# Third edge stage of a four-layer graph kernel: three engine programs as loops over the row buffers

## The chip, the cores and the metric

The kernel runs on one core of a Trainium2 chip. The time is that of one execution on the device, in microseconds (us), as the median of several runs. Five engines work side by side, each through its own list of instructions: TensorE (PE, matrix products), VectorE (DVE), ScalarE (ACT), GpSimd (POOL, which issues the gathers here) and SyncE (SP, which issues plain transfers). They meet only at semaphores: one adds to a counter, another waits until the counter has a value. An engine has a sequencer, which reads instructions and handles register arithmetic, branches and some waits itself, and a datapath behind it.

## The reference, cut to what matters

A graph has 6,250 nodes of 128 channels and 206,250 edges, sorted by target node. Four layers follow one another. The change touches the edge part of the third one:

```
h = relu(layernorm(x))                                  # 6250 x 128
xs, xv = h[:, :32] @ W_up0, (h[:, 32:] as 32x3) @ W_up1 # node tables
emb = radial basis of edge_weight                       # 8 numbers an edge
w = silu(silu(emb @ w0 + b0) @ w1 + b1) @ w2 + b2       # 4 x 32 weights an edge
Y = sqrt(3) * edge_vec / |edge_vec|
m0 = w0 * xs[src];  m1 = w1 * xs[src] * Y
m2 = w2 * xv[src];  m3 = w3 * <xv[src], Y> / sqrt(3)
sums over the edges of each dst of (m0, m3) and of (m1, m2)   # 256 numbers a node
```

## The kernel before, in words

The kernel is written engine by engine, with the semaphores set by hand; nothing reorders it. Edges are taken in tiles of 128 and groups of U = 4 tiles. There are EDGE_GROUPS = 403 groups. `table2` in device memory has a row of 128 numbers for each node. R = 4 row buffers hold the gathered rows of a group each, so that group n uses buffer r = n mod 4 and turn g = n div 4 of the buffers.

For every group n of the third edge stage:

- SP (L1607) waits until the messages of group n-4 are done (`s_mid`, which starts at 4) and loads the radial basis of the group into `base`. Its program is already a loop over the turns (`ring`, L90).
- POOL (L1618) waits for the same count and issues four indirect gathers, one for each tile, into `rows` (L1623).
- TensorE, `radial` (L1695): `w0` times `base` (L1699), the bias product (L1700), `w1` times `h1` (L1703), then four products with `w2` that give the edge weights in `psW` (L1707). It does so for group n+2 while it sums group n: `sums` (L1710) multiplies `mid` with the one-hot matrix `hot`, two products for each of the four tiles (L1714), into `psS`. Products in f32 stand as several instructions, each with a load of weights ahead of it.
- ScalarE (L1631): two Silu operations, `h1` (L1633) and `h2` (L1635), each between two products of TensorE.
- VectorE, `messages` (L1652), for group n+1: the one-hot matrix `hot` (L193), the products and sums that give `mid` (L1664 to L1680), and between them the four `add`s of group n (L1650): each reads the sums of a tile from `psS` and adds them to `ACC` at the window of 128 nodes that begins with the tile's first dst. These four node numbers are loaded into registers (L200), and the place in `ACC` is worked out in registers.

So the sums of group n on TensorE need `mid` of group n and `hot` of group n from VectorE, and the adds of group n on VectorE need these sums. The program of TensorE runs `step` (L1717) for n = 0 to 402, after `radial` for groups 0 and 1; that of VectorE runs `messages(0)` and then its `step` (L1682).

The words `ring` and `straight` are two helpers. Both call `step(n, g, r)` for every n. In `straight` (L110) n is a Python number, so that the program has 403 copies of the step, one behind the other, with constants as the values to wait for and as the addresses. In `ring` (L90) there is one loop over g on the engine, whose body has 4 copies of the step, for r = 0 to 3. There n and g come from a register. As 403 is 4 x 100 + 3, the loop makes 100 turns and three steps stand behind it.

Of the kernel before, what the change touches and what calls it, by code (L numbers as in the profile page):

```python
# [26 lines left out]
EDGE_GROUPS = -(-E // (P * U))  # L27
# [62 lines left out]
def ring(eng, total, slots, step):  # L90

    with eng.Fori(0, total // slots) as g:
        for r in range(slots):
            step(slots * g + r, g, r)
    for n in range(total - total % slots, total):
        step(n, n // slots, n % slots)
# [13 lines left out]
def straight(total, slots, step):  # L110

    for n in range(total):
        step(n, n // slots, n % slots)
# [7 lines left out]
def build(nc, a, out):  # L121
# [19 lines left out]
    with ctx:  # L141
# [9 lines left out]
        def alloc(stack):  # L151
# [12 lines left out]
            return sb, ps, sem  # L164

        sb, _, _ = alloc(ctx)

        def pool_sems(name, n):
# [29 lines left out]
        def windows(eng, tile):  # L198

            _, firsts = nc.values_load_multi_w_load_instructions(  # L200
                D0[0:1, bass.ds(tile, U)], engines=(eng.engine,), min_val=0, max_val=N,
                skip_runtime_bounds_check_because="a dst is a node number, and padding edges end at N")
            return firsts
# [368 lines left out]
        with ExitStack() as st:  # L572
            sb, ps, sem = alloc(st)
            R0 = H * B0
            R = 3
# [330 lines left out]
        with spanning:  # L906
# [4 lines left out]
            with second:  # L911
# [131 lines left out]
                with ExitStack() as st:  # L1043
                    sb, ps, sem = alloc(st)
                    R = 3
# [436 lines left out]
            with third:  # L1482
# [99 lines left out]
                with ExitStack() as st:  # L1582
                    sb, ps, sem = alloc(st)
                    R = 4
# [17 lines left out]
                    with nc.Block() as block:  # L1602
# [26 lines left out]
                        @block.scalar  # L1629
                        def _(act):  # L1630
                            def silus(n, g, r):  # L1631
                                act.wait_ge(s_h0, n + 1)
                                nc.scalar.activation(h1[:, :], psA[:, 0, :], ACT.Silu, bias=b01[:, 0:1]).then_inc(s_h1, 1)  # L1633
                                act.wait_ge(s_h1p, n + 1)
                                nc.scalar.activation(h2[:, r % 2, :], psA[:, 1, :], ACT.Silu, bias=b01[:, 1:2]).then_inc(s_h2, 1)  # L1635

                            straight(EDGE_GROUPS, R, silus)

                        @block.vector
                        def _(dve):  # L1640
# [48 lines left out]
                                    messages(n + 1, g if r < R - 1 else g + 1, (r + 1) % R, n)  # L1689

                            messages(0, 0, 0)
                            straight(EDGE_GROUPS, R, step)

                        @block.tensor
                        def _(pe):  # L1695
                            def radial(n, g, r, between=(lambda: None, lambda: None)):

                                pe.wait_ge(s_base[r], 16 * g + 16)
                                nc.tensor.matmul(psA[:, 0, :], w0[:, :], base[:, r, :], start=True, stop=True).then_inc(s_h0, 1)  # L1699
                                nc.tensor.matmul(psW[:, r % 2, :, :], three[:, :], b2row[:, :].unsqueeze(1).to_broadcast([P, U, P]), start=True, stop=False)  # L1700
                                between[0]()
                                pe.wait_ge(s_h1, n + 1)
                                nc.tensor.matmul(psA[:, 1, :], w1[:, :], h1[:, :], start=True, stop=True).then_inc(s_h1p, 1)  # L1703
                                between[1]()
                                pe.wait_ge(s_h2, n + 1)
                                for u in range(U):
                                    done = nc.tensor.matmul(psW[:, r % 2, u, :], h2[:, r % 2, (u % 2) * P:(u % 2 + 1) * P], w2[:, u // 2, :], start=False, stop=u == U - 1)  # L1707
                                done.then_inc(s_w, 1)

                            def sums(n, r, tiles):  # L1710
                                for u in tiles:
                                    pe.wait_ge(s_free, n * U + (u + 1))
                                    for b in range(2):
                                        done = nc.tensor.matmul(psS[:, u, b, 0:P], mid[:, r % 2, u, b * C:(b + 1) * C], hot[:, r % 2, u, :], start=True, stop=True)  # L1714
                                    done.then_inc(s_sum, 1)

                            def step(n, g, r):  # L1717
                                pe.wait_ge(s_hot, n + 1)
                                pe.wait_ge(s_mid, n + (R + 1))
                                if isinstance(n, int) and n + 2 > last:  # L1720
                                    sums(n, r, range(U))
                                else:
                                    radial(n + 2, g if r < R - 2 else g + 1, (r + 2) % R,
                                           (lambda: sums(n, r, range(0, U // 2)), lambda: sums(n, r, range(U // 2, U))))

                            radial(0, 0, 0)
                            radial(1, 0, 1)
                            straight(EDGE_GROUPS, R, step)


        closing = ExitStack()
        with closing:
# [56 lines left out]
            with ExitStack() as st:  # L1789
                sb, ps, sem = alloc(st)  # L1790
                R = 4
# [393 lines left out]
```

## Time and profile before

| | us |
|---|---|
| median of 3 runs | 11154.02 (11152.67 to 11200.2) |
| the profiled execution, its own time | 11197.17 |
| its span, first to last instruction | 11195.4 |
| from 5898 to 8614 us: the third edge stage | 2716 |
| TensorE busy in that stretch | 2069.93 |
| VectorE busy in that stretch | 1827.50 |
| GpSimd busy in that stretch | 1583.76 |
| ScalarE busy in that stretch | 382.88 |

The times are in microseconds from the start of the span. Register, branch and semaphore instructions, and the issue of a transfer, are not counted as busy. "PE" is a matrix product and "PEld" a load of weights; the start of a product is recorded and its end is modelled. A clock (PEclk) of 1.00 is the higher of TensorE's two levels, 2.4 GHz, and 0.50 the lower one, 1.2 GHz. A row of waits names who was idle, on which tile and line, and what seems to have ended the idle time. Where that is "DMA HN" or "DMA relB" within this stage, the name comes from another stage that used the same semaphore, and "remote" and "issue" name nobody. A number of packets in a queue called "instruction" is that of the blocks of code which engines read from device memory.

### The profile page before, as it was taken

The numbers are of one execution on the slowest core, as the hardware profiler recorded it, in microseconds if no ns is written. First come the engines' busy times: TensorE is split into PE (matmuls) and PEld (weight loads), VectorE is DVE, ScalarE is ACT, GpSimd is POOL, SyncE is SP. The second block draws the span as 40 slices with busy tenths as digits, with TensorE's granted clock in tenths as the row PEclk, the third lists the DMA queues.
The fourth block names the chain that finished last, engine by engine and source line by source line (L and its number), as shares of the span: only waits on it lengthen the run. The fifth ranks groups of instructions, "written<-read, shape, count | busy, mean of one in ns | idle before, by whom it ended". The sixth has DMA issues, their size and how long they took to land. (4 is left out here: it accounts for less than half of the span.)

```text
span 11195.4 us, 158258 instructions
## 1 busy us (share of the span) xinstructions
PE 7512.2 (67%) x45679; PEld 5676.2 (51%) x45679; DVE 6853.5 (61%) x18737; ACT 4365.1 (39%) x7367; POOL 7061.2 (63%) x6167
## 2 busy tenths in 40 slices
PE   1333333335899998998956777777777677777775
PEld 1322322333666666666645666666666344444443
DVE  3555555566677777666655666666666444444445
ACT  1111121121667776666621111111111566666664
POOL 3666666662688888888855555556554655555554
PEclk5555555556889999999977888888888788888887
DMA  4434434442666666777761111111111111111111
GB/s 118 110 96 105 111 98 104 101 97 65 103 106 106 107 106 109 109 109 109 110 117 46 43 43 43 43 42 43 42 42 46 45 43 44 44 44 45 44 44 43
DMA packets 1068830, 846.48 MB, mean 76 GB/s; under 512 B 404136, under 2 KB 907183, under 8 KB 1067542
## 3 DMA queue, kind: packets, MB, share of 16 engines
q0 software_dynamic: 360512, 407.88, 20.9%
q1 hardware_dynamic: 676812, 313.54, 12.7%
q10 hardware_dynamic: 30652, 115.04, 3.1%
q8 instruction: 368, 6.03, 0.2%
q14 instruction: 486, 3.98, 0.1%
HBM read 696.14 MB, written 139.60 MB: 75 GB/s over the span
## 5 line engine op out<-in xcount | busy, mean ns | idle before, releaser
L1474 POOL DMA_INDIRECT sums<-sumrows,index x1460 | 2458.1, 1684 | 694.3 <-issue 348.9
L1623 POOL DMA_INDIRECT rows<-table,index x1612 | 1583.8, 982 | 1128.8 <-DVE mid L1680 582.1
L679 POOL DMA_INDIRECT rows<-table,index x1612 | 1609.3, 998 | 1015.9 <-issue 692.0
L1873 POOL DMA_INDIRECT ACC<-table,index x1472 | 1398.4, 950 | 1129.2 <-DVEq L1998 615.1
L1650 DVE TENSOR_TENSOR ACC<-ACC,psS 128x256 f32 x1612 | 674.6, 418 | 792.1 <-PE psS L1714 471.2
L1714 PEld LDWEIGHTS psS<-hot,mid 128*128 128x128 f32 x6448 | 1042.9, 230 | 57.7 <-issue 3.0
L1714 PE MATMUL psS<-hot,mid 128*128 128x128 f32 x6448 | 1032.2, 313 | 2.7 <-DVE mid L1680 2.3
L2045 PE MATMUL psG<-limbs,pickA 128*128 128x384 bf16 x4060 | 902.1, 355 | 159.4 <-issue 102.7
L1910 ACT ACTIVATE pickA<-apart,K 128x512 bf16<-128x512 bf16 x1015 | 721.2, 711 | 717.2 <-remote 475.0
L1966 DVE TENSOR_TENSOR pickD<-ACC,psK 128x512 bf16<-128x512 f32 x700 | 459.9, 682 | 746.4 <-remote 545.4
L1421 PE MATMUL psB<-pickD,limbs 128*128 128x512 bf16 (+1 forms) x2964 | 824.5, 391 | 81.5 <-DVE pickD L1288 77.0
L1421 PE MATMUL psB<-pickA,limbs 128*128 128x512 bf16 (+1 forms) x2964 | 820.9, 389 | 28.1 <-ACT pickA L1355 24.1
L1954 DVE TENSOR_TENSOR ACC<-ACC,psS 128x128 f32 x1612 | 464.1, 288 | 470.7 <-remote 188.9
L1903 ACT ACTIVATE apart<-ACC,lows 128x512 bf16<-128x512 f32 x1015 | 732.4, 722 | 33.5
L1707 PE MATMUL psW<-w,h 128*128 128x128 f32 x3224 | 503.0, 305 | 351.4 <-ACT h L1635 205.1
L2045 PE MATMUL psG<-limbs,pickD 128*128 128x384 bf16 x2800 | 651.2, 350 | 119.3 <-issue 116.1
L1633 ACT ACTIVATE h<-psA,b 128x256 f32<-128x256 f32 x403 | 190.7, 473 | 1319.8 <-PE psA L1699 775.0
L2045 PEld LDWEIGHTS psG<-limbs,pickA 128*128 128x128 bf16 x4060 | 415.2, 105 | 484.8 <-issue 210.1
L1347 ACT ACTIVATE apart<-steps,away 128x512 bf16<-128x512 int16 (+1 forms) x988 | 646.5, 694 | 7.0
L1707 PEld LDWEIGHTS psW<-w,h 128*128 128x128 f32 x3224 | 454.1, 217 | 379.5 <-ACT h L1635 220.3
L829 DVE TENSOR_TENSOR ACC<-ACC,psA 128x128 f32 x1612 | 465.7, 289 | 286.5 <-issue 101.2
L1355 ACT ACTIVATE pickA<-apart,K 128x512 bf16<-128x512 bf16 (+1 forms) x988 | 638.5, 684 | 0.1
(349 smaller groups left out, 15303.0 us busy)
## 6 DMA issues: line engine op xcount, KB each, us to landing
win<-table SPq DMA_DIRECT2D x1612, 64.5 KB
srow<-src_f SPq DMA_DIRECT2D x365, 256.0 KB
HN<-rel_f ACTq DMA_DIRECT2D x102, 512.0 KB
relB<-rel_f ACTq DMA_DIRECT2D x102, 512.0 KB
rows<-table,index POOLq DMA_INDIRECT x3224
er<-limbs SPq DMA_DIRECT2D x1632, 3.0 KB
ACC<-table,index POOLq DMA_INDIRECT x1472
sums<-sumrows,index POOLq DMA_INDIRECT x1460
```

Of the source, the lines that this page charges most:

```text
L679: nc.gpsimd.indirect_dma_start(out=rows[:, r, k, :], out_offset=None, in_=table0[:, :], in_offset=bass.IndirectOffsetOnAxis(ap=index[:, n ...
L1347: nc.scalar.activation(apart[:, at % 2, 0:size], steps16[:, 0:size], ACT.Abs, bias=away[:, m % 2, u, j:j + 1], scale=-1.0).then_inc(s_apar ...
L1421: last = nc.tensor.matmul(psB[:, c % 2, 0:size], limbs[:, m % 2, k, u, :], chosen, start=u == 0 and k == 0, stop=u == U - 1 and k == 2)
L1474: nc.gpsimd.indirect_dma_start(out=sums1[u][:, :], in_=sums[:, n % 2, u, :], in_offset=None, compute_op=ALU.add, out_offset=bass.IndirectO ...
L1623: nc.gpsimd.indirect_dma_start(out=rows[:, n % R, u, :], out_offset=None, in_=table2[:, :], in_offset=bass.IndirectOffsetOnAxis(ap=index[: ...
L1650: nc.vector.tensor_tensor(own, own, psS[:, u, :, 0:P], ALU.add).then_inc(s_free, 1)
L1707: done = nc.tensor.matmul(psW[:, r % 2, u, :], h2[:, r % 2, (u % 2) * P:(u % 2 + 1) * P], w2[:, u // 2, :], start=False, stop=u == U - 1)
L1714: done = nc.tensor.matmul(psS[:, u, b, 0:P], mid[:, r % 2, u, b * C:(b + 1) * C], hot[:, r % 2, u, :], start=True, stop=True)
L1873: nc.gpsimd.indirect_dma_start(out=rows[:, n % R, u, :], out_offset=None, in_=table3[:, :], in_offset=bass.IndirectOffsetOnAxis(ap=index[: ...
L1903: nc.scalar.activation(apart[:, at % 2, :], names[:, m % 2, :], ACT.Abs, bias=lows[:, onA[k]:onA[k] + 1]).then_inc(s_apart, 1)
L1910: nc.scalar.activation(pickA[:, at % RING, :], apart[:, at % 2, :], ACT.Relu, bias=K[:, C1:C1 + 1], scale=-1.0).then_inc(s_pickA, 1)
L2045: done = nc.tensor.matmul(psG[:, u, 0:3 * C], chosen[:, u * P:(u + 1) * P], limbs[:, b, :], start=b == 0, stop=b == TN - 1)
```

## The change

In the third edge stage, and only there, the programs of TensorE, VectorE and ScalarE call `ring` in place of `straight`. SP's was a loop before. POOL's stays written out. The arithmetic, the tiles and the order of the products are the same.

```diff
@@ ScalarE
-                            straight(EDGE_GROUPS, R, silus)
+                            ring(act, EDGE_GROUPS, R, silus)
@@ VectorE
                             messages(0, 0, 0)
-                            straight(EDGE_GROUPS, R, step)
+                            ring(dve, EDGE_GROUPS, R, step)
@@ TensorE
                             radial(0, 0, 0)
                             radial(1, 0, 1)
-                            straight(EDGE_GROUPS, R, step)
+                            ring(pe, EDGE_GROUPS, R, step)
```

The rows below are instructions in the order of the program, with the line, the operation and the tiles. An ISA row is several register operations in one instruction, a REGISTER_ALU row is one of them; plain waits for semaphores have no row of their own. On VectorE, the start of a group before:

```order
L193 TENSOR_TENSOR hot<-K,REL 128x512
L1664 TENSOR_TENSOR dot<-rows,unit 128x384
L200 TENSOR_LOAD D
L1667 TENSOR_TENSOR q_2<-psW,rows 128x128
L1650 ISA
L1650 TENSOR_TENSOR ACC<-ACC,psS 128x2x128
L1670 TENSOR_TENSOR dot<-dot 128x4x32
```

and in the changed program, from the top of the loop to just ahead of the same first add:

```order
L92 ISA
L193 TENSOR_TENSOR hot<-K,REL 128x512
L1656 ISA
L1663 REGISTER_ALU
L1664 ISA
L1664 TENSOR_TENSOR dot<-rows,unit 128x384
L200 ISA
L200 TENSOR_LOAD D
L1666 REGISTER_ALU
L1667 TENSOR_TENSOR q_2<-psW,rows 128x128
L1647 REGISTER_ALU
L1648 REGISTER_ALU
```

Behind these come the same ISA row and add of L1650. Values to wait for (L1663, L1666, L1647, L1648) and addresses (L193, L1664, L200) are now worked out on the way. From the `L92 ISA` row to the branch at the end the body has 131 rows. Its end, with the first row behind it:

```order
L1678 TENSOR_TENSOR mid<-psW,rows 128x4x32
L1680 TENSOR_TENSOR mid<-psW,dot 128x4x32
L1648 REGISTER_ALU
L1650 ISA
L1650 TENSOR_TENSOR ACC<-ACC,psS 128x2x128
L92 REGISTER_ALU
L92 COMPARE_AND_BRANCH
```

On TensorE, a group before and the end of the body now; "x4" and "x2" are products with nothing between them:

```order
L1699 MATMUL psA<-base,w_2 128x256
L1700 MATMUL psW<-b2row,three 128x512
L1714 MATMUL psS<-hot,mid 128x128 x4
L1703 MATMUL psA<-h_2,w_2 128x256
L1714 MATMUL psS<-hot,mid 128x128 x4
L1707 MATMUL psW<-w_2,h_2 128x128 x4
```

```order
L1712 REGISTER_ALU
L1714 MATMUL psS<-hot,mid 128x128 x2
L1707 MATMUL psW<-w_2,h_2 128x128 x4
L92 REGISTER_ALU
L92 COMPARE_AND_BRANCH
```

The products keep their order; register rows stand between them (28 rows of registers and branch in the body), and a branch behind the fourth group. On ScalarE the body has 15 rows; its top is

```order
L92 ISA
L1633 ACT_TABLE_LOAD
L1633 ACTIVATE h_2<-psA,b_2 128x256
L1635 ACTIVATE h_2<-psA,b_2 128x256
L1632 REGISTER_ALU
```

Before, the load of the activation table stood once, ahead of the first Silu. Now it stands at the top of the body, and so is issued in each of the 100 turns.

## Rows read from the trace of the kernel before

**Rows 1.** Busy time by windows, third edge stage: PE, PEld, DVE, ACT, POOL, PEclk, DMA
```profile
5898.00:8614.00 2716.00, 2069.93 (x11687) 1737.54 (x11687) 1827.50 (x5241) 382.88 (x807) 1583.76 (x1612) 0.83 0.16 43
```
**Rows 2.** Groups of instructions there: count, busy us, mean ns, idle before and releaser
```profile
L1623 POOL DMA_INDIRECT rows<-table,index x1612 | 1583.8, 982 | 1128.8 <-DVE mid L1680 582.1 <-issue 524.0 <-DMA index<-in_src_cols 22.7
...
L1714 PE MATMUL psS<-hot,mid 128*128 128x128 f32 x6448 | 1032.2, 313 | 2.7 <-DVE mid L1680 2.3 <-issue 0.4
L1650 DVE TENSOR_TENSOR ACC<-ACC,psS 128x256 f32 x1612 | 674.6, 418 | 792.1 <-PE psS L1714 471.2 <-DMA HN<-rel_f 260.4 <-issue 54.2
...
L1633 ACT ACTIVATE h<-psA,b 128x256 f32<-128x256 f32 x403 | 190.7, 473 | 1319.8 <-PE psA L1699 775.0 <-remote 308.9 <-issue 236.0
```
**Rows 3.** Waits in that stretch: total us, times, longest us
```profile
POOL rows L1623 <- DVE mid L1680: 582.1, 188, 7.8
...
DVE ACC L1650 <- PE psS L1714: 471.2, 393, 4.8
...
DVE ACC L1650 <- DMA HN<-rel_f: 260.4, 204, 6.2
...
DVE ACC L1650 <- issue: 54.2, 88, 3.4
```
**Rows 4.** Timeline, three groups: start, us, what, idle before
```profile
7003.96 0.69 DVE L193 TENSOR_TENSOR hot<-K,REL 128x512 f32<-128x512 f32 x1
...
7004.64 1.05 PE L1714 MATMUL psS<-hot,mid 128*128 128x128 f32 x8
...
7007.65 0.42 DVE L1650 TENSOR_TENSOR ACC<-ACC,psS 128x256 f32 x1 [2.33 <-PE psS L1714]
...
7012.32 0.69 DVE L193 TENSOR_TENSOR hot<-K,REL 128x512 f32<-128x512 f32 x1
...
7013.70 1.92 PE L1714 MATMUL psS<-hot,mid 128*128 128x128 f32 x8
...
7018.64 0.68 DVE L193 TENSOR_TENSOR hot<-K,REL 128x512 f32<-128x512 f32 x1
...
7023.65 0.69 DVE L193 TENSOR_TENSOR hot<-K,REL 128x512 f32<-128x512 f32 x1
```
**Rows 5.** Windows in and between these groups, columns as in rows 1
```profile
7000.00:7004.00 4.00, 3.61 (x28) 3.37 (x29) 3.69 (x13) 0.95 (x2) 3.08 (x4) 1.00 0.16 41
...
7012.00:7018.00 6.00, 5.82 (x22) 4.93 (x23) 4.32 (x13) 0.95 (x2) 3.84 (x4) 0.50 0.13 36
```
**Rows 6.** SP's loop, line L92: instructions in the queue, ns min/median/max
```profile
L92 SPq FUSED_REGOPS  x100: 2/50/716, 5899.2 to 8543.3; - x100
L92 SPq ALU_OP  x100: 8/33/712, 5901.6 to 8569.6; - x100
L92 SPq COMPARE_BRANCH  x100: 3/45/698, 5901.7 to 8569.7; - x100
```
**Rows 7.** The page: its head, and the queues of code (packets, MB, share)
```profile
span 11195.4 us, 158258 instructions
...
q8 instruction: 368, 6.03, 0.2%
q14 instruction: 486, 3.98, 0.1%
```
**Rows 8.** The same two queues in the stage, 5898 to 8614 us
```profile
q8 instruction: 93, 1.52, 0.2%
q14 instruction: 94, 0.77, 0.1%
```
**Rows 9.** Issues of the whole program: KB each, median us from issue to landing
```profile
WX<-in_L_gnn_lin_w SPq DMA_DIRECT2D x2, 64.0 KB, 1.9
...
WT<-in_L_gnn_W ACTq DMA_DIRECT2D x1, 64.0 KB, 3.2
```
**Rows 10.** TensorE's own wait at a group's start, line L1698, ns min/median/max
```profile
L1698 PEldq EVENT_SEMAPHORE  x401: 406/1535/4653, 5912.7 to 8596.7; - x134
```
**Rows 11.** Groups of instructions of line L1633: the table load
```profile
L1633 ACT ACT_TABLE_LOAD x1 | 1.3, 1283 | 12.9 <-PEq L144 12.9
```

## The prediction

> **What bounds the kernel now.** I read the busy time by windows first, for the stage that the change touches. It lasts 2716 us for 403 groups, 6.74 us a group, and no engine fills it: TensorE 2070 us (76%), VectorE 1828 (67%), GpSimd 1584 (58%), ScalarE 383 (14%). TensorE's granted clock is 0.83 there, so it has the lower level, 1.2 GHz, for about a third of the time [rows 1].
>
> The groups of instructions and the waits tell what the idle time is. GpSimd needs 982 ns for a gather and 524.0/1612 = 0.33 us between two, so 4 x 1.31 = 5.23 us a group, and it waits for VectorE's `mid` 188 times, 582 us in all [rows 2, 3]. It is a floor of 403 x 5.23 = 2110 us, but not the bound. VectorE idles almost only ahead of its adds: 471 + 260 + 54 = 786 us, in 393 + 204 + 88 = 685 waits [rows 3]. In program order only the sums of L1714 can hold an add, so all three names stand for them. TensorE idles for `mid` and for ScalarE. So the bound is a circle: `mid` of VectorE, sums of TensorE, adds of VectorE, `mid` of the next group. Whatever delays either engine at a group's start delays all of it.
>
> The timeline shows that the groups differ. From 7018.64 to 7023.65 one takes 5.0 us. The one from 7003.96 takes 8.4: TensorE's sums are recorded from 7004.64, as fast as ever, but VectorE's add gets its first result so late that it starts at 7007.65, after 2.33 us. I can't say from this why. The next one, from 7012.32, takes 6.3 us with the sums at 1.92 us in place of 1.05 [rows 4]. Its window has a clock of 0.50, where 7000 to 7004 has 1.00 [rows 5]. So a late circle leaves TensorE idle, the clock falls, and the next group is slow as well.
>
> **The change part by part.** Values and arithmetic stay. Four things change.
>
> *Register instructions.* In the body VectorE has 131 instructions for four groups. Before, it had 18 rows a group in the order, and five plain waits which that list leaves out. Nearly all of the new ones come ahead of waits, while VectorE's datapath still works on what it has: between an add and the next add there are 0.6 to 1.6 us of queued operations. What can't hide is the register work of L1648 and L1650 behind a late result. SP's loop shows a register operation at 33 ns and a fused one at 50 [rows 6]. I take 0.05 us for each of the 685 waits that something ended late: 34 us. It is 0 if GpSimd's floor takes it, and 685 x 0.1 = 69 us at most. TensorE's register rows stand between products whose waits sit in the queue, and it is ahead: it waits a median of 1535 ns for `mid` at a group's start, and 406 at the least [rows 10]. Seven or so of 33 to 50 ns are 0.3 us and hide there: nothing, or 403 x 0.1 = 40 us without that cover.
>
> *The branch back.* SP's costs 45 + 33 + 50 ns, 0.13 us a turn [rows 6], but its body is short, four loads with their registers. The question is whether the top of the body is still in the engine when the branch goes there. The code comes from device memory in blocks: 6.03 MB in 368 packets is 16.4 KB each (q8), 3.98 MB in 486 is 8.2 KB (q14), and together 10.0 MB over 158,258 instructions is 63 bytes each [rows 7]. TensorE alone can need the large ones: 2 x 11,687 products and loads of weights in the stage are 58 a group [rows 1], 23,374 in all, and 93 packets of q8 at 16.4 KB and 63 bytes hold 24,200 [rows 8]. So VectorE's body of 131 instructions is 8.3 KB, a little more than its block, and TensorE's, 4 x 58 and 28 more, is 260 instructions and 16.4 KB, a block again. Both cross from one block into another in each turn, wherever they start. The code comes in order now, and no trace here shows an engine going back over a block's edge. If the next block takes the place of the one that the branch goes back to, it must be read again while the engine stands still. The price is then that of a small transfer: 1.9 us is the shortest of the 64 KB ones, 3.2 another [rows 9].
>
> The Trainium skill has both halves of this ("Runtime: NRT & Kernel Launch", on instruction fetch mechanics). A taken branch whose target is outside the two pages that the engine holds must wait for a DMA fetch. But it gives TensorE 128 KB and the others 32 KB, and by these sizes both bodies would fit. The packets of 8.2 KB in this trace are half of its 16 KB page. By its sizes the result would be my first rival, by its window of two pages it depends on where the prefetch stands.
>
> For VectorE I take 1.9 + 0.13 and subtract the add that still runs when the branch is read, 0.42 us [rows 2]: 1.6 us a turn. For TensorE it is 1.9 to 3.2 less its lead of 1.5 [rows 10], so 0.5 to 1.8, and at the same moment, since its next step needs the `mid` that VectorE has just finished. Side by side they cost 1.6 a turn, 160 us in 100 turns. The ends are 100 x 0.13 = 13 us (nothing is read again) and 100 x (3.2 + 0.13) = 333 us with no cover at all.
>
> *The clock.* An idle TensorE at each turn's end meets the lower level more often. Such a group takes 6.3 us against 5.0 [rows 4]. If the fall comes in addition in 60 of 100 turns, as many already fall without it, that is 60 x 1.3 = 78 us. The ends are 0 and 100 x (8.4 - 5.0) less the 1.6 of stall, 180 us.
>
> *ScalarE's table load*, 1283 ns [rows 11], now in every turn. ScalarE is idle 1319.8/403 = 3.3 us ahead of each first Silu [rows 2], and the load doesn't wait for TensorE. The idle time hides it: nothing. Without the cover it would be 128 us.
>
> *What goes.* 187 blocks of straight code [rows 8]. No wait names them, VectorE has no idle time elsewhere than at its adds, and if code is read again there are more packets, not fewer. Nothing; at best a tenth of a microsecond each, -19 us.
>
> Sum: 34 + 160 + 78 = 272 us. The profiled execution took 11197.17 us, 1.8 more than its span, and would take 11469. It stands 43 us above the median of 11154, near the slowest of the three; I add to the median: 11426, so 11430 us (+2.5%).
>
> **The rivals.** *Both bodies stay in the engine.* For it: SP's loop has no long branch at the median, a body is only just over a block, and two blocks may well be held. Against it: nothing in this trace. The registers and 0.13 us a turn remain, 34 + 13 = 47 us: 11200. This is the case to which the Trainium skill's memory sizes lead.
>
> *Two stalls in a row.* If TensorE's reload doesn't lie beside VectorE's, because one waits for the other's first result, a turn costs 1.6 + 1.8 = 3.4 us, and with the upper ends of the clock (180) and registers (69): 340 + 249 = 590 us, 11740. For it: the circle. Against it: TensorE comes to its branch 1.5 us early.
>
> *Faster, through the late sums.* The group of 8.4 us waits for results that TensorE seems to have made. If that hangs on the pattern of waits in TensorE's queue, which register instructions now break up, or on the reading of code, fewer groups would be late. GpSimd's floor allows 2716 - 2110 = 606 us at most. A fifth of it, 120 us, less 47: 11080. It decides from 47 us saved, which is 14 late groups of 3.4 us. For it: the cause is open. Against it: late groups come every three to four groups, code blocks of TensorE every 2716/93 = 29 us [rows 8], which is 4.3 groups.
>
> **How the numbers follow.** Reload with overlap 0.50, resident bodies 0.27, stalls in a row 0.13, faster 0.10. A measurement of this kernel tells 0.5%, 56 us, from no change. Resident bodies at +47 with 0 to 120 us fall on both sides: 0.17 within, 0.10 above. So faster 0.10, the same 0.17, slower 0.73. The forecast's own range is 11290 (13 + 34 + the clock, with a reload mostly covered) to 11620. The range for all reaches down to the resident case and up towards the second rival: 11180 to 11700.
>
> **What would show it.** Reload: q8 in the stage at 200 packets or more and q14 at 200 or more, in place of 93 and 94; on VectorE an idle time of 1 to 2 us ahead of L193 in every fourth group, where the idle time now is nearly all ahead of L1650; PEclk in the stage below 0.83. Resident: fewer than 20 packets in both together, and idle time only ahead of L1650. Stalls in a row: TensorE idle ahead of L1699 for over 3 us in every fourth group. The registers: more idle time ahead of L1650, in shares of 0.05 us. The table load: 101 of them at 1.28 us, with ScalarE's L1633 never late by it. I would be wrong if the stage got shorter than 2716 us, or if the idle time sat at every group and not at every fourth.

## The result, and the profile after

The changed kernel took 11286.2 us (median of 4 runs, 11265.24 to 11305.74). The kernel before, run beside it, took 11165.69 us (4 runs, 11152.67 to 11200.2). The ratio is 1.0100, with a 95% interval of 1.0082 to 1.0118: 120 us slower by the medians, 92 to 132 by that interval. The forecast was slower by 272 us. The sign was right, the size was more than twice too large, and the step that made it large, the reading of code at each branch back, did not take place. The time lies inside the forecast range (11180 to 11700).

The page's head and its two queues of code answer to [rows 7]:

```profile
span 11268.0 us, 165461 instructions
...
q8 instruction: 277, 4.54, 0.2%
q14 instruction: 409, 3.35, 0.1%
```

There are 7203 instructions more in the trace, and 168 packets of code fewer. The same two queues within the stage, 5898 to 8687 us, answer to [rows 8]:

```profile
q14 instruction: 17, 0.14, 0.0%
q8 instruction: 2, 0.03, 0.0%
```

93 and 94 packets have become 2 and 17. The prediction asked for fewer than 20 in both together if the bodies stay in the engines, and for 200 in each queue if they are read again. It is the first: 19.

Busy time by windows (PE, PEld, DVE, ACT, POOL, PEclk, DMA share, GB/s) for the part ahead of the stage, the stage, and the part behind it; the second row answers to [rows 1]:

```profile
0.00:5898.00 5898.00, 3575.01 (x23425) 2727.30 (x23426) 3754.34 (x10613) 2454.91 (x4116) 4087.22 (x3103) 0.75 0.56 105
5898.00:8687.00 2789.00, 2124.21 (x11640) 1776.12 (x11638) 1818.83 (x5222) 505.93 (x899) 1561.31 (x1593) 0.82 0.15 40
8687.00:11268.00 2581.00, 1856.82 (x10616) 1210.03 (x10616) 1277.91 (x2904) 1531.89 (x2451) 1397.39 (x1472) 0.83 0.17 45
```

The part behind the stage is as long as it was (11195.4 - 8614 = 2581 us). The stage takes more. Its window holds 401 of the 403 groups (VectorE's `hot` is counted below), so a group takes 2789/401 = 6.96 us, against 6.74: 0.22 us by 403 groups is 89 us. Measured between the starts of L1664, from the first group to the last, it is 6.965 against 6.698 us, 107 us. The spans differ by only 73 us, because in this profiled execution the stage begins 30 us earlier (5868 in place of 5898), in work that the change doesn't touch. The profiled execution also had the highest mean granted clock of the four (0.782, the others 0.774 to 0.777).

Groups of instructions in the stage (count, busy us, mean ns, idle before and what ended it) answer to [rows 2] and [rows 11]:

```profile
L1623 POOL DMA_INDIRECT rows<-table,index x1593 | 1561.3, 980 | 1211.4 <-DVE mid L1680 699.4 <-issue 512.0
...
L1714 PE MATMUL psS<-hot,mid 128*128 128x128 f32 x6432 | 1051.8, 318 | 2.7 <-DVE mid L1680 2.3 <-issue 0.4
L1650 DVE TENSOR_TENSOR ACC<-ACC,psS 128x256 f32 x1610 | 667.9, 415 | 744.0 <-PE psS L1714 407.0 <-DMA HN<-rel_f 236.4 <-issue 95.1
...
L193 DVE TENSOR_TENSOR hot<-K,REL 128x512 f32<-128x512 f32 x401 | 274.3, 684 | 1.6
...
L1633 ACT ACTIVATE h<-psA,b 128x256 f32<-128x256 f32 x400 | 189.4, 474 | 1382.5 <-PE psA L1699 654.2 <-remote 592.5 <-issue 135.8
...
L1633 ACT ACT_TABLE_LOAD x99 | 127.0, 1283 | 1.8
L1667 DVE TENSOR_TENSOR q<-psW,rows 128x128 f32<-128x128 f32 x401 | 114.0, 284 | 227.5 <-DMA relB<-rel_f 223.2 <-PE psW L1707 2.8 <-issue 1.4
```

Of the kernel before, the row of L1667 in its stage and its wait:

```profile
L1667 DVE TENSOR_TENSOR q<-psW,rows 128x128 f32<-128x128 f32 x403 | 116.1, 288 | 77.7 <-DMA relB<-rel_f 70.9 <-PE psW L1707 4.6 <-issue 1.2
```
```profile
DVE q L1667 <- DMA relB<-rel_f: 70.9, 31, 5.5
```

Read these rows on VectorE, which holds the circle. Ahead of `hot` (L193), the first operation behind a branch back, it idles for 1.6 us in this window: there is no stall there. Ahead of the adds (L1650) it idles less than before, 744 us against 792. What is new stands ahead of L1667, the first product that needs TensorE's `psW`: 227.5 us, where before it was 77.7. The name of a DMA there is the profile's guess; by the program that wait is for TensorE's L1707. VectorE's idle time in the stage was about 893 us (792.1 + 77.7 + 14.2 + 8.7). Over the whole stage of the changed kernel, from 5868 us on, it is 1001 (749.9 + 227.5 + 13.5 + 10.3). The difference, 108 us, is the 107 us by which the stage is longer. So the loss is waiting for TensorE's results, and it stands in the groups of all four positions in a turn: between starts of L1664 they took 6.66, 6.85, 6.55 and 6.73 us before and take 6.81, 7.07, 7.01 and 6.98. A cost of the branch would stand in one of the four.

The load of ScalarE's table takes 1283 ns in each turn, and costs nothing that this row shows.

The waits of the stage answer to [rows 3]:

```profile
POOL rows L1623 <- DVE mid L1680: 699.4, 201, 6.3
...
DVE ACC L1650 <- PE psS L1714: 407.0, 319, 4.2
...
DVE ACC L1650 <- DMA HN<-rel_f: 236.4, 149, 7.3
DVE q L1667 <- DMA relB<-rel_f: 223.2, 120, 4.7
...
DVE ACC L1650 <- issue: 95.1, 139, 2.8
```

Late adds number 319 + 149 + 139 = 607 in place of 685, late L1667s 120 (31 before, 70.9 us). The timeline (start, us, what, idle before) shows one such group, to be read beside [rows 4]:

```profile
7022.99 0.69 DVE L193 TENSOR_TENSOR hot<-K,REL 128x512 f32<-128x512 f32 x1
7023.60 0.55 DVE L1664 TENSOR_TENSOR dot<-rows,unit 128x384 f32<-128x384 f32 x1
7023.71 1.05 PE L1714 MATMUL psS<-hot,mid 128*128 128x128 f32 x8
7027.31 0.29 DVE L1667 TENSOR_TENSOR q<-psW,rows 128x128 f32<-128x128 f32 x1 [3.15 <-DMA relB<-rel_f]
7027.35 0.47 ACT L1633 ACTIVATE h<-psA,b 128x256 f32<-128x256 f32 x1 [6.27 <-remote]
...
7027.88 1.22 PE L1703 MATMUL psA<-h,w 128*128 128x256 f32 x2 [3.11 <-issue]
7028.90 1.91 PE L1714 MATMUL psS<-hot,mid 128*128 128x128 f32 x8
```

TensorE's sums are recorded from 7023.71 at full pace. Yet VectorE and ScalarE both go on with results that they need from it only at 7027.3, within 0.04 us of each other. Then the granted clock is at its lower level (0.50 between 7028 and 7032), and eight products take 1.91 us. It is like the late group of the kernel before, but the results for L1667 and the first Silu, which were on time there, are late here as well.

The register work is now seen directly. Instructions of the queue (ns: min/median/max) at L92 answer to [rows 6], and the two lines of an add stand with them:

```profile
L92 PEldq COMPARE_BRANCH  x100: 76/208/233, 5920.4 to 8673.1; - x100
L92 DVEq ALU_OP  x100: 40/40/40, 5921.4 to 8674.4; - x100
L92 DVEq COMPARE_BRANCH  x100: 50/56/73, 5921.5 to 8674.5; - x100
...
L92 DVEq FUSED_REGOPS  x99: 98/98/98, 5921.8 to 8649.7; - x99
...
L1648 DVEq ALU_OP  x1598: 40/40/40, 5901.9 to 8673.5; - x200
...
L1650 DVEq FUSED_REGOPS  x1610: 46/46/53, 5901.9 to 8686.1; - x179
```

VectorE's branch costs 56 + 98 + 40 = 0.19 us a turn, and each add has one register operation more, the 40 ns of L1648; the 46 ns of L1650 were there before. TensorE's wait at a group's start [rows 10] now stands in several instructions of its queue, so its lead can't be read in the same way.

### The profile page after: what moved, and what is told of

Its sections match the earlier page's. It is cut to its first block and busy times, and to the rows that moved or that the text cites. A ratio compares the mean times of both kernels' runs of the same rounds, so it can differ in the third digit from the quotient of the medians.

```text
span 11268.0 us, 165461 instructions
## 1 busy us (share of the span) xinstructions
PE 7556.0 (67%) x45679; PEld 5713.4 (51%) x45679; DVE 6851.1 (61%) x18738; ACT 4492.7 (40%) x7466; POOL 7045.9 (63%) x6167
## 5 line engine op out<-in xcount | busy, mean ns | idle before, releaser
L1650 DVE TENSOR_TENSOR ACC<-ACC,psS 128x256 f32 x1612 | 668.8, 415 | 749.9 <-PE psS L1714 407.0
L1714 PEld LDWEIGHTS psS<-hot,mid 128*128 128x128 f32 x6448 | 1068.1, 235 | 62.1 <-issue 3.0
L1714 PE MATMUL psS<-hot,mid 128*128 128x128 f32 x6448 | 1055.6, 318 | 2.7 <-DVE mid L1680 2.3
L1633 ACT ACTIVATE h<-psA,b 128x256 f32<-128x256 f32 x403 | 190.8, 474 | 1393.8 <-PE psA L1699 658.8
L1707 PE MATMUL psW<-w,h 128*128 128x128 f32 x3224 | 517.9, 312 | 216.0 <-ACT h L1635 172.5
L2018 PE MATMUL psS<-ACC 128*128 128x128 f32 x2944 | 480.5, 306 | 181.8 <-issue 114.1
```

What stands on the lines that cost most here:

```text
L1650: nc.vector.tensor_tensor(own, own, psS[:, u, :, 0:P], ALU.add).then_inc(s_free, 1)
```

## The experiments

e1 to e8 ran on chips on which the kernel before takes about 9460 us; the first measurement and e9 to e18 on chips where it takes 11154 to 11306. Each ratio is to the kernel before on the same chip, beside the run. The record gives one chip number to e9 to e15, yet the kernel before took 11306 us beside e9 to e12 and 11167 beside e13 to e15; so ratios are compared, and times only within a group of runs.

**e1 to e5: which program, and does it cost everywhere?** Each line of the change alone, then the whole:

```
e1, e4:  -  straight(EDGE_GROUPS, R, step)      +  ring(pe, EDGE_GROUPS, R, step)
e2, e4:  -  straight(EDGE_GROUPS, R, step)      +  ring(dve, EDGE_GROUPS, R, step)
e3:      -  straight(EDGE_GROUPS, R, silus)     +  ring(act, EDGE_GROUPS, R, silus)
e5:      all three, the changed kernel
```

> Only TensorE's program is a loop; VectorE's and ScalarE's stay written out. All three loops together cost 120 us. Theory T (what TensorE's sequencer now does between products, and a wait that moved from the sequencer into the queue, shift its late results so that the clock falls more often): +70 to +110 us, with more time at the lower clock in the stage. Rival V (register work of VectorE behind late sums): 0 to +20. Rival A (the table load in each turn of ScalarE): 0. On record: register rows of TensorE hide, so 0 to +40.

> Only VectorE's program is a loop. Theory V: 34 to 69 us for the register operations behind late sums, as on record, up to +110 if they are all there is. Theory T: 0 to +20. Theory A: 0. If VectorE reads its code again at each branch: over 190 packets of q14 in the stage; the changed kernel had 17, so I expect under 20.

> Only ScalarE's program is a loop, with the activation table's load in each turn (1283 ns). Theory A: the load makes the first Silu of a turn late, +60 to +120 us. Theories T and V, and what is on record (3.3 us of idle time cover it): within 10 us of before.

> TensorE's and VectorE's programs are loops, ScalarE's stays written out: the changed kernel without the table loads. Theories T and V: +100 to +120 us, as much as the changed kernel. Theory A: 0 to +40. If the three costs only arise together, this tells whether ScalarE's has a part.

> The changed kernel once more, beside a kernel before on the same chip. In the runs of e1 to e4 the kernel before took 9459 us and its third edge stage went at GpSimd's pace, 5.04 us a group. Theory G (the cost of the loops only shows where VectorE and TensorE are the bound, through results of TensorE that come late; where the gathers are, they cover it): if the kernel before takes about 9460 here, the ratio is 0.999 to 1.002; if it takes about 11160, the ratio is about 1.01 and the groups with late results are there. Rival S (the +120 us are the sum of three programs' costs wherever it runs): +100 us at either level.

Measured: 1.0006 (0.9996 to 1.0015), 1.0009 (1.0000 to 1.0019), 1.0004 (0.9995 to 1.0014), 1.0006 (0.9996 to 1.0015), and 0.9991 (0.9980 to 1.0003) for the whole change. None costs a clearly measurable amount here. The stage of e1 and a part of e5's (windows, columns as above) and e5's waits of GpSimd say why:

```profile
5430.00:7480.00 2050.00, 1688.22 (x11687) 1443.06 (x11687) 1799.39 (x5240) 381.95 (x807) 1542.46 (x1612) 0.99 0.21 56
```
```profile
5480.00:7400.00 1920.00, 1568.77 (x11035) 1341.38 (x11034) 1747.17 (x4947) 482.97 (x856) 1455.94 (x1523) 1.00 0.21 55
```
```profile
POOL rows L1623 <- issue: 464.4, 1523, 0.3
```

The same stage takes 2050 us in place of 2716. The clock stays up, no result is late, and in e5 GpSimd's only idle time is its 0.3 us between two gathers (1523 times, never longer, never for `mid`). In e1 `mid` is named 326 times, never for more than 0.3 us. A group takes 5.05 us, and GpSimd's own work is 4 x (956 + 305) ns, 5.04 us. That is the floor that the prediction named (at 5.23 us, by gathers of 982 ns), here reached, and it hides the loops.

**e6 and e7: the bare toll.** The gathers of the stage are left out from group 4 on, so the sums read old rows and GpSimd sets no pace. e6 does it to the kernel before, e7 to the changed one.

```
-  for n in range(EDGE_GROUPS):                  +  for n in range(R):
-  dve.wait_ge(s_rows[r], 16 * U * g + 16 * U)   +  dve.wait_ge(s_rows[r], 16 * U)
```

> The kernel before with the gathers of the third edge stage left out from group 4 on (the four row buffers keep the rows of groups 0 to 3; the output isn't the reference's). GpSimd's floor of 5.04 us a group is gone, so the stage goes at the pace of the circle of VectorE and TensorE. Where TensorE's results are on time: 4.4 to 4.7 us a group, about 0.4 us less, 9300 us in all. If late results come from the gathers' transfers, none are left here, even where the kernel before takes 11160 us.

> The same with all three loops. Without the gathers' floor the bare cost of the loops can be seen against e6: by what is on record for registers and branches 34 + 13 = 47 us (0.12 us a group); if the load of the activation table shows, more at one group in four. Rival: nothing, since register work hides in both engines' queues. With theory S it would be 100 us.

Measured: 9242.77 us (ratio 0.9757, 0.9738 to 0.9776) and 9282.72 (0.9800, 0.9782 to 0.9819). The medians differ by 40 us, the groups (between starts of L1664) by 4.607 - 4.495 = 0.112 us, 45 us in all, spread over the four positions (4.594, 4.617, 4.569, 4.647). The prediction had put 34 + 13 = 47 us on registers and the branch without a reload. The sum agrees by luck: it was 0.05 us for each of 685 late waits, and here no result is late.

**e8 and e12: when does a body no longer stay?** All gathers are present; the three loops run over 16 groups in a turn (e8, 25 turns) and over 8 (e12, 50 turns, `turns=2`).

```
+  def long_ring(eng, total, slots, step, turns=4):
+      whole = total // (slots * turns)
+      with eng.Fori(0, whole) as k:
+          for i in range(slots * turns):
+              step(slots * turns * k + i, turns * k + i // slots, i % slots)
```

> The three loops with 16 groups in a body and 25 turns: VectorE's body has 506 instructions, 32 KB, TensorE's over 1000. The changed kernel read 17 + 2 blocks of code in the stage, so bodies of 8.4 and 16.8 KB stay in the engines. If 32 KB don't stay, q14 has 25 x 4 = 100 packets or more in the stage, and each branch shows its price as idle time ahead of L193: 1.9 to 3.2 us by what is on record. If they stay, under 25. The time: within 0.3% of the kernel before either way where the gathers are the bound.

> All gathers present; the three loops run over eight groups in a turn (two rounds of the row buffers), 50 turns, so that VectorE's body is twice as long as in the changed kernel, about 16 KB, and half as long as in the kernel with sixteen groups in a turn, which showed 155 packets of code on VectorE's queue and 2.57 us a branch ahead of the hot sum. If 16 KB still stays in the engine: fewer than 20 packets on that queue within the stage, no idle ahead of the hot sum, and the time of the kernel before within 0.1%. If it doesn't: 100 or more packets, 50 branches by about 2.6 us or 130 us of idle, of which GpSimd's pace hides most as it did with 25 branches: plus 0.2 to 0.7%.

e8: 1.0024 (1.0015 to 1.0034). Code queues and the `hot` (L203 there), 5480 to 7400 us:

```profile
q14 instruction: 155, 1.27, 0.2%
q8 instruction: 3, 0.05, 0.0%
```
```profile
L203 DVE TENSOR_TENSOR hot<-K,REL 128x512 f32<-128x512 f32 x376 | 256.0, 681 | 59.3 <-issue 59.3
```

Here the reload exists: 155 packets of 8.2 KB in that stretch, and 59.3 us of idle time ahead of the first operation behind the branch, 2.6 us for each of 23 turns. VectorE's body is 506 instructions, 32 KB at the 63 bytes of the prediction's count; TensorE's, twice as long, is not read again (3 packets). The stalls also bring the clock down: PEclk is 0.96 in that window, where e5 has 1.00, and 22 stretches at the lower level begin in it, in e5 none.

```profile
5480.00:7400.00 1920.00, 1612.61 (x10904) 1379.21 (x10903) 1688.12 (x4888) 385.89 (x775) 1461.63 (x1505) 0.96 0.21 55
```

e12 ran where results come late: 1.0100 (1.0079 to 1.0121), where 0.1% had been expected of a body that stays. Its rows for 5898 to 8700 us:

```profile
q14 instruction: 18, 0.15, 0.0%
q8 instruction: 2, 0.03, 0.0%
```
```profile
L203 DVE TENSOR_TENSOR hot<-K,REL 128x512 f32<-128x512 f32 x388 | 267.1, 688 | 9.9 <-PEq L154 8.7
```

With 256 instructions, 16 KB, VectorE's body stays. So the size of the body decides, with the limit between 16 and 32 KB for VectorE. And with half as many branches the kernel is about as much slower as with all of them (113 us by its ratio, 89 to 137, against 112 in the first measurement and 138 in e17): most of what it pays doesn't count turns, as half of it would be 56 to 69 us. A share of 10 us, half of VectorE's 0.19 us a turn, is too small to be seen in it.

**e9 to e11: whose toll?** The edit of e6, and one of the three loops in each.

> Leaves out the gathers of the third row stage from group 4 on (the sums read old rows), so that GpSimd's gathers no longer set the pace; of the three programs only VectorE's is a loop. The straight form without those gathers took 9243 us and 4.495 us a group, the form with three loops 9283 us and 4.607 us. Theory one, the toll is VectorE's registers (eight of its waits a group now compare with a register, and an update of one costs 40 ns or more ahead of a sum that follows at once): 4.58 to 4.61 us a group and 9275 to 9285 us. Theory two, the toll is TensorE's (its records show the longer wait, 190 us ahead of L1699 in place of few): 4.49 to 4.52 us a group and 9240 to 9255 us. Shared evenly: 4.54 and 9260 us.

> Leaves out the same gathers; only TensorE's program is a loop. Theory one (VectorE's registers carry the toll): 4.49 to 4.52 us a group, 9240 to 9255 us. Theory two (TensorE's registers and its branch back of 208 ns carry it): 4.58 to 4.61 us a group, 9275 to 9285 us. If both are on the one chain through the recurrence of buffers, the two kernels add to the whole: about 4.55 each.

> Leaves out the same gathers; only ScalarE's program is a loop, with its table load of 1.283 us in every turn. If the load is hidden in ScalarE's idle time, as predicted: 4.49 to 4.51 us a group, 9240 to 9252 us. If it is on the path once a turn: 1.28 us by 100 turns, 128 us at most, 9370 us, with the longer period in one of every four groups.

Measured: 10391.64, 10362.8 and 10369.05 us, with 4.611, 4.540 and 4.516 us between starts of L1664. The absolute times can't be held against e6's, which came from another chip, and these means can't either: each holds one group of 11 to 13 us at the start of the stage, where gathers are still there, and e6 has none. Without the first ten groups they are 4.583, 4.514 and 4.492 us, against 4.489 in e6 and 4.601 in e7. The written-out form on a chip of this kind (e18, below, no late results either) has 4.492, so the comparison between the chips holds. VectorE's loop makes most of the difference of 0.112 us: 0.094, or 38 us in 403 groups. TensorE's makes 0.025 (10 us) and ScalarE's 0.003 (1 us), and the three add up to 0.122. The expectations of e13 and e14 still took 0.116 and 0.045 from the means. The window of e6 and VectorE's wait for sums in it (5460 to 7200 us), then the same of e9 (5930 to 7740):

```profile
5460.00:7200.00 1740.00, 1588.43 (x11244) 1367.53 (x11242) 1711.38 (x5039) 367.23 (x775) 5.32 (x6) 1.00 0.02 5
```
```profile
DVE ACC L1650 <- PE psS L1714: 2.3, 6, 0.4
```
```profile
5930.00:7740.00 1810.00, 1618.25 (x11449) 1392.95 (x11449) 1747.72 (x5132) 374.07 (x790) 0.00 (x0) 1.00 0.02 4
```
```profile
DVE ACC L1650 <- PE psS L1714: 48.8, 297, 0.5
```

VectorE was 98% busy in e6 (1711.38 of 1740 us), so its register operations ahead of the adds show as gaps: 48.8 us over 395 groups is 0.12 us a group, enough for the 0.094. Two more things stand in that window: without gathers nothing is late, on a chip of the kind where with them some 30% of the groups are (in the trace of the kernel before 119 of 397 groups have a wait of VectorE over 2 us), and the granted clock is 1.00.

**e13, e14 and e16: one loop each, all gathers, late results present.** The kernels of e2, e1 and e3 once more.

> Only VectorE's program is a loop, all gathers present: asked again because the earlier answer came from a chip where GpSimd's pace of 5.04 us a group hid everything; on the chips where TensorE's results come late (6.7 us a group) the changed kernel pays 120 us. Without the late results VectorE's loop alone carries the whole bare toll (4.611 us a group against 4.607 with three loops and 4.495 with none). Theory one, the toll of 0.11 us a group on VectorE is what is given back more than twice where results come late: plus 0.8 to 1.2% (90 to 135 us). Theory two, the toll is passed on as it is: plus 0.4% (45 us), and the other 70 us belong to TensorE's or ScalarE's loop. On a chip with no late results: within 0.1%.

> Only TensorE's program is a loop, all gathers present. Theory one: its bare toll is 0.045 us a group (4.540 against 4.495), so plus 0.15 to 0.4% (18 to 45 us). Theory two, the lateness itself depends on TensorE's program (its waits stand in the instruction stream as register work in place of constants): plus 0.6% or more (70 us). On a chip with no late results: within 0.1%.

> Only ScalarE's program is a loop, all gathers present. VectorE's loop alone measured plus 0.73% (0.46 to 1.00) and TensorE's plus 0.44% (0.27 to 0.61) on a chip where TensorE's results come late; together 130 us, against 120 us for all three. Theory one, the shares add up and nothing is left for ScalarE: within 0.2% (its table load of 1.283 us stays hidden). Theory two, its own register waits (two a group, each often the last to end) cost too: plus 0.2 to 0.5%. On a chip with no late results: within 0.1%.

| kernel | ratio (95%) | us | bare toll, us |
|---|---|---|---|
| VectorE's loop (e13) | 1.0073 (1.0046 to 1.0100) | 81 | 38 |
| TensorE's loop (e14) | 1.0044 (1.0027 to 1.0061) | 49 | 10 |
| ScalarE's loop (e16) | 1.0007 (0.9995 to 1.0020) | 8 | 1 |
| all three (first, e17) | 1.0100, 1.0122 | 112, 138 | 45 |

The us are the ratio by the kernel before on that chip, the bare toll is the difference of e9, e10, e11 and e7 to e6's 4.489 us a group, by 403. ScalarE's table load and its waits cost nothing that can be measured. VectorE and TensorE each pay some 40 us more than their bare toll, and these shares add: 0.73 + 0.44 + 0.07 = 1.24%.

**e15: a mere delay in VectorE's program.** No loops; two fills of a 128x1 tile more in each group.

```
+  nc.vector.memset(fill[:, 0:1], 0.0)     ahead of add(before, firsts, 0)
+  nc.vector.memset(fill[:, 1:2], 0.0)     ahead of add(before, firsts, 2)
```

> No loops; VectorE's program has two fills of 128x1 more in each group (a fill of 128x1 took 59 ns in the trace of before, so 0.118 us a group, the bare toll of VectorE's loop), one ahead of the first late sum and one ahead of the third. Theory one, it is the delay that counts, whatever makes it: the same as with VectorE's loop alone, plus 0.8 to 1.2% where results come late. Theory two, the delay is passed on as it is: 47 us, plus 0.4%. Theory three, only the loops' registers and branch do it: within 0.2%. On a chip with no late results: within 0.1%, hidden by GpSimd's pace.

Measured: 1.0038 (1.0024 to 1.0051), 42 us of the 47 put in. This delay is passed on as it is. It isn't multiplied, so theory one fell, and VectorE's loop seems to cost more (81 us) than a delay of some 40 us; the two intervals overlap a little (51 to 112 us, 27 to 57 us), so this alone doesn't prove it. Against their bare tolls, VectorE's loop (51 us or more, bare 38), TensorE's (30 to 68 us, bare 10) and all three (92 us or more, bare 45) do cost more. One rival is not tested: the fills stand at two places of VectorE's program, the register operations ahead of every wait of two engines, and the place of a delay may matter as much as its kind.

**e17: the changed kernel on e16's chip.**

> All three loops and all gathers, the changed kernel, on one chip with ScalarE's loop alone. If the shares add up (81 us VectorE, 49 us TensorE, about nothing ScalarE): plus 1.0 to 1.3% (115 to 145 us) where results come late. If the loops overlap in their cost: plus 0.7 to 0.9%. On a chip with no late results: within 0.1%.

Measured: 1.0122 (1.0103 to 1.0140), as the sum of the shares foretold. Its waits, 5880 to 8700 us, repeat the first result's, and behind them stand those of TensorE's loop alone (e14, same stretch):

```profile
POOL rows L1623 <- DVE mid L1680: 748.6, 186, 6.1
...
DVE q L1667 <- DMA relB<-rel_f: 328.8, 137, 4.8
```
```profile
DVE ACC L1650 <- PE psS L1714: 426.9, 262, 4.5
DVE ACC L1650 <- DMA HN<-rel_f: 267.5, 156, 6.9
DVE ACC L1650 <- issue: 169.1, 201, 4.0
DVE q L1667 <- DMA relB<-rel_f: 54.7, 27, 5.4
```

In the same stretch the wait of L1667 is 101.5 us (80 times) with VectorE's loop alone and 54.7 (27 times) with TensorE's alone, no more than before; only together do they make it large. What TensorE's loop costs alone stands ahead of the adds: 426.9 + 267.5 + 169.1 = 864 us, against 786 before.

**e18: half of the gathers.** From group 4 on two of each group's four are left out, in the kernel before (those tiles read old rows).

```
-  for u in range(U):      +  for u in range(U if n < R else U // 2):
```

> Leaves out two of the four gathers of each group from group 4 on (those tiles read old rows); no loops. Where TensorE's results come late with all gathers (6.70 us a group) and never with none (4.5 us): if each gather is what makes the results late, half of them leave about half of the lateness, 5.4 to 5.8 us a group, 10640 to 10800 us; if the lateness needs GpSimd to be busy nearly all the time, it goes: 4.5 to 4.7 us a group, about 10340 us, with the granted clock at 1.00 through the stage. On a chip with no late results: 4.50 us a group, as with none.

Measured: 10363.02 us, 0.9182 (0.9166 to 0.9198). The stage's window:

```profile
5930.00:7700.00 1770.00, 1614.14 (x11429) 1389.47 (x11428) 1741.71 (x5124) 374.00 (x789) 809.92 (x788) 1.00 0.13 34
```

The lateness goes altogether with half of the gathers, not by half: 4.49 us a group, the clock at 1.00, where all gathers make 6.7 in the trace of the kernel before (between starts of L1664). GpSimd is busy for 46% of that window. Leaving out 798 gathers saved 929 us.

## Why the prediction was wrong

**What bounds the kernel** was read rightly: the circle of `mid`, sums and adds, with late results in it. GpSimd's floor was right too, if a little high (5.23 us a group, 5.04 in e5), and e1 to e5 stand on it.

**The branch back** is the step that failed: 160 of the 272 us, "if the next block takes the place of the one that the branch goes back to". It doesn't: 19 packets of code in the stage, 1.6 us of idle time ahead of L193. The error was to take a body that crosses a block's edge for one that must be fetched; bodies of two blocks and more are held. The stall itself exists, and had the right order of size, 2.6 us a turn in e8 against 1.6 assumed. On VectorE a body of 16 KB doesn't bring it and one of 32 KB does. The Trainium skill ("Runtime: NRT & Kernel Launch", on instruction fetch mechanics) gives 32 KB to VectorE and 128 KB to TensorE, and a stall when the target lies outside what is held. In the runs 8 and 16 KB stayed, 32 KB on VectorE did not, and TensorE's 64 KB did. These runs agree with the sizes for TensorE and for the short bodies, and I should have given them more than 0.27. The body of 32 KB (506 instructions by 63 bytes, 31.9 KB) would just have fitted by the size alone and was read again all the same; a block read ahead may take part of the room, which is not shown. What remains of the branch, 0.19 us a turn on VectorE, is 19 us at most. TensorE's, 208 + 50 + 32 ns, is 0.29 us a turn, where I had taken SP's 0.13.

**The registers** were put at 34 us, or 47 with the branch. Their bare cost is 45 us (e7 against e6), and 38 of it VectorE's, as said; but that agreement is luck, since it comes from the gaps ahead of adds with VectorE otherwise full, and not from late waits. For TensorE I took nothing, because it waits 1.5 us for `mid`: bare it is 10 us, which the cover nearly explains, but where results come late it is 49, above the 40 that I gave it without any cover. Why is not shown.

**The clock** was put at 78 us for 60 more falls at the branches. In the traces, between the first start of L1664 and the last, the lower level was granted for 889 us in 127 stretches before, and for 1020 us in 152 after. Work of TensorE at that level takes up to twice as long (eight products of L1714 took 1.05 us at the one and 1.91 at the other), so 131 us of it give back up to 65 us. That is the size of what is missing between 45 and 120 us, so this term was nearly right in size. Where a branch does stall, as in e8, the clock falls with it; here nothing stalls at the branch, so the mechanism of the term failed with the reload.

Nor does the clock tell the loops from a mere delay. The record has the mean granted clock of every run, and twice its distance from 1, by the span, is the time at the lower level in the whole program. It is longer than in the kernel before, run beside, by 78 us with e15's fills, 69 with TensorE's loop, 128 with VectorE's, 15 with ScalarE's and 219 with all three (e17). These are 1.4 to 1.9 times the losses of 42, 49, 81, 8 and 138 us. More time at the lower level goes with every loss, and these runs can't say which of the two makes the other. So the part above the bare toll, some 65 to 95 us of all three loops' cost, stays without a shown cause. Where it sits is known: in waits for TensorE's results, ahead of L1667 and the first Silu with all three loops, ahead of the adds with TensorE's alone.

**The table load** at nothing: right, within what e11 and e16 can tell. **The blocks of code gone** at nothing: e1 to e5 agree.

**The rivals.** "Both bodies stay in the engine" was the right mechanism, at 47 us, and is what a chip without late results would show if GpSimd didn't hide it. "Two stalls in a row" fell with the reload. "Faster, through the late sums" was wrong in sign: of 397 groups, 119 had a wait of VectorE over 2 us before and 125 have one now, and those with one over 3 us went from 28 to 54. About as many groups are late, and some are later. The last sentence of the prediction named what would refute it, idle time at every group, and that is what came.

## What to carry to other kernels

A loop on an engine costs code fetches only when its body is larger than the engine holds: count the body's instructions by 63 bytes, and look at the packets of the code queues within the stage. Below that size it costs register operations of 32 to 98 ns at waits and addresses, which show in the time of an engine that has no idle time to hide them (VectorE here, 0.09 us a group) and not where another engine sets the pace. Leave out the first groups of a stage when you compare periods that differ by hundredths of a microsecond. Before putting a price on a wait, find out whether the same kernel on another chip shows that wait at all.

## What the runs showed of the hardware

- **The same program differs by 18 to 20% between chips.** The kernel before takes 9459 and 9469 us on two, and 11154 to 11306 on the others. On the slow ones TensorE's results can reach the other engines some 4 us after its products are recorded (the first Silu at 7027.35 in the late group above, its products recorded to 7023.55). In about 30% of the groups VectorE waits over 2 us, and the stage has 127 stretches at the lower clock, where the stage of e5 has next to none.
- **These late results need the gathers, and not in proportion.** On the slow chips they come with all four gathers a group (GpSimd busy for 58% of the stage); with two, or none, no group of the windows shown was late. The other chips do all four, with GpSimd busy for 75% of the stage (e1), and nothing is late. What connects the two was not found.
- **A branch back has a different price on each engine:** at the median the compare-and-branch takes 45 ns on SP and ScalarE, 56 on VectorE and 208 on TensorE.
- **The table of ScalarE's function is loaded again in every turn of a loop,** 1283 ns each, though it never changes; no kernel here was measurably slower by it.
